# Tail and order of a routed expert stage in a Perceiver block: sorted slots, earlier gathers, Silu ahead of the copy

## The reference

```python
logits = x @ gate_weight.T            # 16 experts
scores = sigmoid(logits); biased = scores + expert_bias
# the 2 best of 4 groups, then the 4 best experts of them
w = take(scores, sel); w = w / (w.sum(-1) + 1e-20) * 2.5
for g, u, d, we in experts:           # hidden size 256
    acc += we[:, None] * ((silu(x @ g.T) * (x @ u.T)) @ d.T)
out = acc + (silu(x @ shared_gate.T) * (x @ shared_up.T)) @ shared_down.T
x = x + out                           # x in the experts is layer-normed
```

## Time and profile before

| | us |
|---|---|
| median of 3 runs | 1574.61 (1571.99 to 1577.38) |
| profiled execution, its own time | 1570.21 |
| its span in the profile | 1568.4 |
| PE / DVE / ACT / GpSimd busy | 1371.3 / 806.7 / 730.2 / 578.3 |
| tile loop, first to last product | about 1250 to 1513 |
| first gather to end of span | 1517.7 to 1568.4 |

### The profile page before, as it was taken

How to read it: one execution, slowest core, us unless ns; L and a number is a source line. 1 busy time by engine, 2 the same in 40 slices (tenths; PEclk the granted TensorE clock), 3 DMA queues, 4 the chain that set the end, 5 groups by cost and what they waited for, 6 DMA issues and landing times. The chain is left out here.

```text
span 1568.4 us, 22740 instructions
## 1 busy us (share of the span) xinstructions
PE 1371.3 (87%) x7136; PEld 1104.5 (70%) x7136; DVE 806.7 (51%) x1361; ACT 730.2 (47%) x1741; POOL 578.3 (37%) x347
## 2 busy tenths in 40 slices
PE   5997799999999999999957999996898899997950
PEld 4775678787878787878736888885786677775730
DVE  4443565757575757575634444444798622222225
ACT  2443464646564646464524777775212133332310
POOL 2212241414141414141022333332465635169726
PEclk9998899999999999999978999996999999999985
DMA  5785720505050505050441111125432444456437
GB/s 218 229 279 158 273 96 1 215 1 214 3 211 4 210 7 207 10 204 27 162 163 68 55 48 64 50 90 185 169 131 81 161 167 143 135 194 236 162 104 218
DMA packets 78984, 209.79 MB, mean 134 GB/s; under 512 B 5888, under 2 KB 39168, under 8 KB 72960
## 3 DMA queue, kind: packets, MB, share of 16 engines
q1 hardware_dynamic: 69472, 163.78, 29.6%
q0 software_dynamic: 7136, 38.80, 7.4%
q10 hardware_dynamic: 2304, 6.29, 1.1%
HBM read 154.59 MB, written 92.01 MB: 157 GB/s over the span
## 5 line engine op out<-in xcount | busy, mean ns | idle before, releaser
L660 DVE TENSOR_TENSOR probsT_lo<-psTr,probsT_hi 128x512 fp32r<-128x512 f32 x256 | 176.5, 690 | 200.4 <-ACT probsT_hi L610 200.1
L610 ACT CAST probsT_hi<-psTr 128x512 fp32r<-128x512 f32 x256 | 149.9, 586 | 211.7 <-PE psTr L750 211.0
L750 PE MATMUL psTr<-ident,probs 128*128 128x128 f32 x1024 | 152.5, 275 | 18.9 <-DVE probsT_lo L660 12.8
L750 PEld LDWEIGHTS psTr<-ident,probs 128*128 128x128 f32 x1024 | 122.2, 141 | 62.2 <-DVE probsT_lo L660 29.1
L655 DVE TENSOR_REDUCE nmax<-psS 128x1 f32<-128x1024 f32 x128 | 155.4, 1214 | 11.2 <-PE psS L66 10.4
L527 POOL TENSOR_TENSOR ctxT_lo<-ctx_f,ctxT_hi 128x512 fp32r<-128x512 f32 x32 | 41.3, 1289 | 321.0 <-ACT ctxT_hi L579 321.0
L572 ACT ACTIVATE probs<-psS,nmax 128x1024 f32<-128x1024 f32 x128 | 143.3, 1120 | 28.3 <-DVE nmax L655 28.3
L64 PE MATMUL bank<-w_slots,ao_first_hi 128*128 (+1 forms) x252 | 107.5, 427 | 20.0 <-DVE w_slots L1724 9.3
L64 PE MATMUL psV<-probsT_hi,kv_hi 128*128 128x512 f32 x256 | 117.3, 458 | 2.0
L64 PE MATMUL psS<-kT_hi,qe 128*128 128x512 f32 x256 | 112.9, 441 | 5.5 <-issue 4.6
L1455 POOL TENSOR_TENSOR w_slots<-w_ahead,w_slots 128x3072 fp32r<-128x3072 f32 x16 | 109.0, 6810 | 1.3
(11 more groups left out here) (269 smaller groups left out, 3428.1 us busy)
## 6 DMA issues: line engine op xcount, KB each, us to landing
w_ahead<-w_exp POOLq DMA_DIRECT2D x14, 1536.0 KB, 7.3
qe<-stage SPq DMA_DIRECT2D x16, 1024.0 KB, 6.8
qe<-qe SPq DMA_DIRECT2D x16, 1024.0 KB, 5.1
wraw<-w_pairs SPq DMA_DIRECT2D x8, 1792.0 KB, 12.1
early<-xs SPq DMA_DIRECT2D x47, 256.0 KB, 2.7
xs<-h_rows SPq DMA_DIRECT2D x47, 256.0 KB, 2.0
early<-ctx SPq DMA_DIRECT2D x16, 512.0 KB, 4.0
ao<-attn_out SPq DMA_DIRECT2D x32, 256.0 KB, 2.4
```

The costliest lines, as they stand in the source:

```text
L610: act.copy(PT[k % PTN].hi[:], psT[slot][:]).then_inc(turned_hi, 1)
L660: dve.tensor_tensor(out, psT[slot][:], f32(hi), ALU.subtract).then_inc(turned_free, 1)
L750: last = pe.transpose(psT[slot][:, q * P:(q + 1) * P], src(q), ident[:])
```

## The change

- ScalarE: in each step of the tile loop, Silu of tile i is issued ahead of the copy of result i - 1.
- SP: six blocks are loaded ahead instead of three, with the same four buffers; load i + 6 is issued behind the store of tile i. After each store SP waits until the one before has landed and then raises a count, y_landed.
- The low part of expert 0 is made on the DVE, between hidden_low(1) and product(2). GpSimd issues the last scatters without that subtract ahead of them, and waits for the tile table only from expert 4 on.
- A new DVE function, sort_slots, is called in step 1 of the tile loop. It sorts each token's four slots (and weights) in ascending order, which is the order of the experts: choice 0 then lies in expert 12 or lower, choice 1 in 13 or lower, choice 2 in 14 or lower.
- GpSimd gathers choice by choice, choice 0 of all eight token tiles first. Before choice k it waits until the tiles of expert 12 + k have landed, before choice 3 for all tiles. There are 24 buffers G, half of them in h3T.
- The DVE makes the first four additions in the loop's last full step and the others behind the loop.

```diff
--- before.py
+++ after.py
...
@@ -1351,7 +1359,10 @@
     ht = h3T.hi[:, 0, :].rearrange("p (j a i x) -> p j a i x", j=2, a=2, i=NIT)
     HT = [(ht[:, j, 0], ht[:, j, 1]) for j in range(2)]
     Y = [HN[:, j, :] for j in range(YR)]
-    G = [ahead[:, j * BANK:(j + 1) * BANK] for j in range(GR)]
+    G = [ahead[:, j * BANK:(j + 1) * BANK] for j in range(2 * wcol // BANK)]
+    G += [f32(h3T.lo[:, k, j * BANK:(j + 1) * BANK]) for k in range(KC) for j in range(T // BANK)]
+    G += [f32(h3T.hi[:, k, j * BANK:(j + 1) * BANK]) for k in range(1, 3) for j in range(T // BANK)]
+    GR = len(G)
 
     rows = t["xs"].rearrange("b p c -> (b p) c")
...
@@ -1411,21 +1425,28 @@
         def block_at(i):
             return sp.value_load(tab[0:1, 2 * NTILE + i:2 * NTILE + i + 1], min_val=0, max_val=NBLK - 1)
 
+        def landed(i):
+            sp.wait_ge(y_out[i % YR], 16 * (i // YR + 1))
+            sp.sem_inc(y_landed, 1)
+
         def load_x(i):
             wait(sp, x_turned, i - XR + 1)
             sp.dma_start(X[i % XR], t["xs"][bass.ds(block_at(i), 1)].rearrange("o p c -> p (o c)")).then_inc(
                 x_in[i % XR], 16)
 
-        for i in range(XR - 1):
+        for i in range(XR + 2):
             load_x(i)
         for i in range(NTILE):
-            if i + XR - 1 < NTILE:
-                load_x(i + XR - 1)
+            if i >= 1:
+                landed(i - 1)
             sp.wait_ge(y_made, i + 1)
             sp.dma_start(t["xs"][bass.ds(block_at(i), 1)].rearrange("o p c -> p (o c)"), Y[i % YR]).then_inc(
                 y_out[i % YR], 16)
+            if i + XR + 2 < NTILE:
+                load_x(i + XR + 2)
+        landed(NTILE - 1)
         for tt in range(NT):
-            sp.wait_ge(comb, TOPK * (tt + 1))
+            sp.wait_ge(comb, NT * (TOPK - 1) + tt + 1)
             sp.dma_start(t["out"][tt], acc[:, tt, :]).then_inc(out_sem, 16)
         sp.wait_ge(out_sem, 16 * NT)
@@ -1474,14 +1495,15 @@
             if tt >= 2:
                 scatter(tt - 2, 2)
                 scatter(tt - 2, 3)
-        pool.wait_ge(e0_hi, 1)
-        expert_low(0)
         for tt in range(NT - 2, NT):
             for k in range(TOPK):
                 scatter(tt, k)
+        pool.wait_ge(e0_lo, 1)
+        pool.sem_inc(w_ready, 1)
         expert_load(2)
-        pool.wait_ge(table_made, 2)
         for e in range(1, NE):
+            if e == NSLOT:
+                pool.wait_ge(table_made, 2)
             if e == 1:
                 pool.wait_ge(raw_in[0], 32)
             else:
@@ -1499,15 +1521,21 @@
             expert_low(e)
             if e + 2 < NE:
                 expert_load(e + 2)
-        for j in range(YR):
-            pool.wait_ge(y_out[j], 16 * len(range(j, NTILE, YR)))
         pool.wait_ge(w_ready, NE)
+        pool.wait_ge(sorted_made, 1)
         for g in range(NT * TOPK):
-            tt, k = g // TOPK, g % TOPK
+            k, tt = g // NT, g % NT
+            if tt == 0:
+                landed = NTILE + 1
+                if k < TOPK - 1:
+                    e = NE - TOPK + k
+                    landed = pool.value_load(cum_i[0:1, e:e + 1], min_val=1, max_val=NTILE + 1)
+                pool.wait_ge(y_landed, landed)
+                pool.sem_inc(gather_free, 1)
             wait(pool, comb, g - GR + 1)
             pool.indirect_dma_start(G[g % GR], None, rows,
-                                    bass.IndirectOffsetOnAxis(ap=pos_i[:, tt, k:k + 1], axis=0)).then_inc(
-                                        g_in[g % GR], 16)
+                                    bass.IndirectOffsetOnAxis(ap=pos_si[:, tt, k:k + 1], axis=0)).then_inc(
+                                        g_in[k] if k < TOPK - 1 else g_last[tt], 16)
 
     @block.scalar
     def _(act):
@@ -1587,10 +1615,10 @@
                 ht_high(i - 1)
             if i + 1 < NTILE:
                 xt_high(i + 1)
+            if i < NTILE:
+                silu(i)
             if i >= 1:
                 y_out_copy(i - 1)
-            if i < NTILE:
-                silu(i)
 
     @block.vector
     def _(dve):
...
@@ -1705,6 +1733,18 @@
             dve.wait_ge(row_mm, 1)
             dve.tensor_copy(tab[:], psR[0][0:1, 0:3 * NTILE]).then_inc(table_made, 1)
 
+        def sort_slots():
+            big = [P, NT, TOPK, TOPK]
+            pj, pi = pos_all[:].unsqueeze(2).to_broadcast(big), pos_all[:].unsqueeze(3).to_broadcast(big)
+            link(dve.tensor_tensor(cmp_k, pj, pi, ALU.is_lt))
+            link(dve.tensor_reduce(rank_k[:], cmp_k, AX.X, ALU.add))
+            for src, dst in ((pos_all, pos_s), (cw, cw_s)):
+                link(dve.tensor_tensor(cmp_k, rank_k[:].unsqueeze(2).to_broadcast(big),
+                                       c_row(C_K, TOPK).unsqueeze(1).unsqueeze(3).to_broadcast(big), ALU.is_equal))
+                link(dve.tensor_tensor(cmp_k, cmp_k, src[:].unsqueeze(2).to_broadcast(big), ALU.mult))
+                link(dve.tensor_reduce(dst[:], cmp_k, AX.X, ALU.add))
+            dve.tensor_copy(pos_si[:], pos_s[:]).then_inc(sorted_made, 1)
+
         def product(m):
             dve.wait_ge(silu_made, m + 1)
             wait(dve, hid_lo, m - 1)
...
@@ -1754,6 +1795,8 @@
         slots(last)
         table_cols()
         hidden_low(1)
+        dve.wait_ge(e0_hi, 1)
+        dve.tensor_tensor(WS[:, wcol:2 * wcol], raw[1], f32(WS[:, 0:wcol]), ALU.subtract).then_inc(e0_lo, 1)
         product(2)
         hidden_low(2)
         product(3)
@@ -1778,6 +1821,16 @@
             dve.tensor_tensor(HT[i % 2][1], psHT[i % 2][:, 0:I].rearrange("p (k x) -> p k x", k=NIT),
                               f32(HT[i % 2][0]), ALU.subtract).then_inc(ht_lo, 1)
 
+        def combine(g):
+            k, tt = g // NT, g % NT
+            if k < TOPK - 1:
+                dve.wait_ge(g_in[k], 16 * NT)
+            else:
+                dve.wait_ge(g_last[tt], 16)
+            wait(dve, comb, g - NT + 1)
+            dve.scalar_tensor_tensor(acc[:, tt, :], G[g % GR], cw_s[:, tt, k:k + 1], acc[:, tt, :], ALU.mult,
+                                     ALU.add).then_inc(comb, 1)
+
         xt_low(0)
         for i in range(NTILE + 1):
             if i >= 1:
@@ -1786,13 +1839,13 @@
                 xt_low(i + 1)
             if i < NTILE:
                 gated(i)
-        for g in range(NT * TOPK):
-            tt, k = g // TOPK, g % TOPK
-            dve.wait_ge(g_in[g % GR], 16 * (g // GR + 1))
-            if k:
-                dve.wait_ge(comb, g)
-            dve.scalar_tensor_tensor(acc[:, tt, :], G[g % GR], cw[:, tt, k:k + 1], acc[:, tt, :], ALU.mult,
-                                     ALU.add).then_inc(comb, 1)
+            if i == 1:
+                sort_slots()
+            if i == NTILE - 1:
+                for g in range(NT // 2):
+                    combine(g)
+        for g in range(NT // 2, NT * TOPK):
+            combine(g)
 
     @block.tensor
     def _(pe):
```

More of the change, by code:

```diff
@@ L1260 @@
 NBLK = NE * NT + DUMMY
-XR, YR, GR, HR = 4, 3, 12, 3
+XR, YR, HR = 4, 3, 3
+G_EARLY = 8 * (TOPK - 1)
 C_BIAS, C_TRI, C_TRIG, C_DIAG = 0, NE, NE + NE * NE, NE + NE * NE + NG * NG
```

29 lines of the change are left out of this document (20 added, 9 removed).

## The result

| | before | after |
|---|---|---|
| median of the runs | 1574.73 us (1571.99 to 1577.38) | 1563.79 us (1562.34 to 1565.96) |
| profiled execution | 1570.21 us | 1564.69 us |
| its span | 1568.4 us | 1562.9 us |
| first and last gather | 1517.66, 1560.24 us | 1480.42, 1554.30 us |

The ratio is 0.9925, with an interval of 0.9903 to 0.9947: faster by 11 us, where 44 were forecast. The sign was right and the size was not; 1563.8 lies far outside 1516 to 1545.

What follows compares the result with a forecast made beforehand. It took a serial tail of 32 gathers behind the last tile as the bound; loop end -13.4 us and 24 gathers moved beside the loop gave a span of 1524.1 from 1568.4, 1530 us as median, range 1516 to 1545.

Steps and rivals of the forecast that it cites:

- three signs of being wrong: First gather after 1480, gathers over 1.8 us apart, or the loop still ending after 1505.
- Start: Router and first tiles: expert 0's low part on the DVE frees the router's comparison; -7.0 us, bounds 4 and 9.3.
- up to 2.3 us back: At hidden_low(3): GpSimd's cast of expert 1 falls behind it, so it no longer takes 3.01 instead of 0.69 us.
- Tile loop: First 26 tiles: Silu ahead of the copy and loads six ahead give 4.85 us per tile, -12.7 us.
- Sort: Tile 2: the sort's DVE operations wait for GpSimd's cast and subtract, PE stands; +9.0 us, bounds +0 and +10.
- The boldest step: Tile 2: one sort operation of 2.7 us, one of about 6.8, PE idle 8 to 9 us once.
- GpSimd's stretch: Experts 8 to 15, paced by GpSimd's conversions: keeps its length and moves with tile 26, by -10.7 us.
- The gathers: Loop's end: 24 gathers run beside the last seven tiles, 1471 to 1503.9; 2 us added for shared DMA engines.
- rival (2): DMA engines fill up: landings stretch, last store late, additions hold up descriptors, 13 us over 32 gathers; 1543, chance 0.22.
- Tail: Behind the loop: choice 3's eight gathers 1.37 us apart, then 4.72, 0.75 and 2.7 us to the end; 17.8 us.

Runs made afterwards that it cites:

- e2: The changed kernel with the sort of the slots in step 5 of the tile loop instead of step 1; 1521.19 us, ratio 0.9662.
- e0: The changed kernel once more, unaltered, on another chip; 1560.67 us, ratio 0.9922.
- f1: The changed kernel with one small GpSimd operation of about 0.6 us ahead of the first gather; 1558.69 us, ratio 0.9905.
- f2: The changed kernel with four small GpSimd operations in a row ahead of the first gather; 1561.8 us, ratio 0.9931.
- g1: The changed kernel with its 24 early gathers three to a tile, each three behind SyncE's issue of that tile's store; 1536.59 us, ratio 0.9751.
- g2: The changed kernel with its early gathers three to a tile, each three waiting for the same signal as SyncE's store issue; 1538.3 us, ratio 0.9771.
- h1: The changed kernel with the sort in step 5, unchanged, run a second time on another chip; 1551.95 us, ratio 0.986.
- e3: The changed kernel with its 24 early gathers in groups of four, each group behind the landing of the one before; 1544.56 us, ratio 0.9808.
- e4: The changed kernel with expert 0's low part back on GpSimd, ahead of the last scatters; 1537.48 us, ratio 0.977.
- g3: The changed kernel with only two choices (16 gathers) early, the third waiting for the loop as the fourth does; 1556.28 us, ratio 0.9883.
- f5: The changed kernel with the sort in step 5 and one small GpSimd operation ahead of the first gather; 1552.57 us, ratio 0.9852.

## Why the prediction was wrong, point by point

On the profile's own scale the forecast was a span of 1524.1 us and it was 1562.9: 38.8 us. Two of the three signs of being wrong that it named came true: the first gather came at 1480.42, just behind 1480, because the small misses ahead of it add up, and the loop ended at 1533 and not before 1505. In order of time:

- **Ahead of the change, +2.6.** The router's code before 1200 us, which the diff leaves alone, ran 2.6 us later than in the profile of before. No step of mine could have it: the same place lies anywhere from 1195.8 to 1206.1 us in the 20 profiles, so it is the spread from run to run.
- **Start, -4.3 in place of -7.0: +2.7.** The comparison was right to the hundredth, and up to the start of hidden_low(3) all 7.0 us are there. The failed half is "up to 2.3 us back": I let expert 1's cast fall behind hidden_low(3), but the scatters moved up and took the cast with them, 1.1 us. The other 1.6 us are TensorE's clock, which fell behind the wait of 3.46 us; I had no term for it. The run that undoes this part alone gives the same 4.1. The value lay inside my bounds (4 to 9.3), and I chose wrongly between them.
- **Tile loop, 4.90 us per tile in place of 4.85: +1.4.** From the sort in step 5: 127.5 us for 26 tiles against 138.8 before, -11.3 where I had -12.7. No wait for a block is left, as forecast.
- **Sort, +10.7 in place of +9.0: +1.7.** The boldest step was right in its mechanism and almost in its size. PE's idle was 8.56 us; the other 2 are behind it, where the granted clock is 0.51 until 1275 and matmuls start 0.43 us apart in place of 0.23. The profiles together put the cost at about 10 us, still nearer to my 9.0. The Trainium skill ("SBUF — State Buffer", Who interferes with whom) calls the ports of VectorE and GpSimd an exclusive lock for the whole instruction. The trace agrees again: 3.24 and 6.69 us for 0.29 us operations.
- **GpSimd's stretch: 0.** Forecast to keep its 83.1 us; it took 83.3 (1395.63 to 1478.98).
- **The gathers, the step that failed: +25.** I wrote that 24 gathers "run ... beside the last seven tiles" and priced that at 2 us for shared DMA engines. The gathers did run so, at 1.26 us. The tiles did not: four of them took 45.2 us in place of 20. My rival (2) looked for contention in the landings and stores. They were on time as far as the trace has them; a store issued at 1486.20 landed 2.0 us later. The price fell on the one link that I gave none, TensorE's signal to ScalarE, up to 24 us late. No row of the kernel before could show it, since no gather there runs beside a matmul; that ought to have made it an unknown cost with a wide bound, not 2 us.
- **Tail, +7.6.** From the first gather of choice 3 to the end of the span 25.4 us in place of 17.8: that gather took 8.11 us and not 0.95 beside the DVE's back-to-back additions. I had this mechanism in rival (2), at 0.4 us for each gather. It doesn't slow each a little; it stops one until the additions end. The Trainium skill (same page, on the bandwidth-pool intuition) says of a DMA of this kind beside a DVE tensor_copy that it is "waiting for descriptors" and not transferring slowly. The operation here is another one, a scalar_tensor_tensor, but the rows look the same: in all six profiles where the gather met the unbroken run of additions (6.05 to 8.11 us) it ends 0.82 or 0.83 us behind the last of them. In e2 the order is the other way: choice 3 waits 3.34 us for the DVE once and its gathers take 1.35 at most.

These make 2.6 + 2.7 + 1.4 + 1.7 + 25 + 7.6 = 41.0, of which 2.2 come back in small terms of the last tiles (the 2 us that I had added for contention among them).

So the forecast held where the profile of before had rows for it. Without the stall the parts add up: the run with the low part on GpSimd, 1537.5 us, less the 4.1 of that part, is 1533.4, an estimate of the kernel after on a chip that doesn't stall, 3 us from the forecast of 1530. **Shown** is that most of the gap is the stall (the same program ran in 1521 and in 1552 us), that it lasts as long as the stream, and that breaks in the stream keep it from costing time. In the kernel after itself that is read from its own rows and from e0; the pair of 1521 and 1552 us is its variant with the sort in step 5. **Open** is what makes it. It is neither the start's place in a tile (f1, f2) nor the collision with SyncE's issues (g1, g2), nor the program alone (h1). It hardly is the chip alone: chip 14 was free of it in the first batch and had it in the fourth, though with another program, of 16 gathers. What is drawn anew between batches, such as where in memory the data lie, wasn't tried.

Nor was a rival that the traces themselves suggest, the recording. Every run here was taken with the profiler at work, and its records thin out where the signals come late. A landed gather should leave 16 records of a rise, the 24 early ones 384. The traces of e2, e3 and e4 have all 384, those of the seven stalls with 24 gathers 60 to 75, and the broken streams of the later batches 189 to 312. No run shows whether the stall comes when nothing is recorded, so a reader shouldn't take the 25 us for the cost of such gathers in an unrecorded kernel.

Both weak points can be mended. With the sort in step 5 it was faster than the kernel before in each batch, 1521.2 us without the stall and 1552.0 with it, and both are below the 1560.7 and 1563.8 of the kernel after. With three gathers to a tile as well it took 1528.3, and with groups of four 1533.7 on a chip that stalls. The breaks cost 7 to 13 us against the free stream of e2 and save 18 to 24 where it stalls.

## What to carry to other kernels

Work that is moved beside another stage isn't hidden because its own rows stay short: look at what the stage beside it lost, and price a pairing that the old profile never shows with a wide bound instead of a small number. Put small DVE operations on SBUF data where GpSimd is idle; one line moved by four tiles was worth about 10 us here. Count what a pause costs behind its end too: 2 of these 10 us were TensorE's clock. And run the same program on another day and chip before you build a theory on a timing: two profiles without the stall and one run that met its forecast had made a false theory look good. Where a wait names no engine, also count the records that the trace should have, before you call it a behaviour of the chip.

## What the runs showed of the hardware

- **TensorE's signals can come late beside a stream of indirect gathers, in recorded runs.** By up to 24 us (after), while matmuls start 0.23 us apart (0.43 once the clock has fallen) until they lack input. ScalarE's first late start is 7.2 to 9.3 us behind the first gather (after, g3, h1), and the delays end with the stream. No recorded signal of ScalarE or of the DVE is late in the kernel after.
- **SyncE's register steps stretch at the same time.** Ahead of a store's issue one takes 0.037 us, and 0.672 us at 1485.5, as the stall begins. Groups of line 1443 in the kernel after and, below, in the free run (ns, least, median, longest):

```profile
L1443 SPq FUSED_REGOPS  x2: 37/354/672, 1485.5 to 1515.7; - x2
```

```profile
L1443 SPq FUSED_REGOPS  x7: 37/37/42, 1467.4 to 1496.6; - x7
```

  A step of 0.19 us or more stands beside the stream in all 13 profiles of the other batches that have early gathers, those with breaks too, and in none of the three of the first batch (e2, e3, e4). Records of TensorE's signals are missing in the stream in 11 of the 13 (all but f1 and f5), those of the DVE and ScalarE in all 13, and none in the three. So something else than the program differed there; that it is the cause isn't shown.
- **A stall that belongs to a batch.** Within a batch all runs of a program agree (1519.4 to 1521.7; 1548.7 to 1554.0), between batches they differ by 31 us, while the kernel before keeps its 1572 to 1574 everywhere.
- **TensorE's clock falls behind a pause.** After 3.46 us and after 8.56 us without work (after) the granted clock went to 0.50 for some 3 and 6 us, after 2.38 us (before, at 1239.64) it stayed at 1.00. It cost 1.6 and 2 us.
- **Back-to-back DVE additions hold up a gather's descriptors to their end.** 8.11 us in place of 0.95 (after), 6.05 to 8.10 in five more runs. With a gap in the additions (e2) no gather took over 1.40 us.
